# Samples of the expert units: loaded by GpSimd as square blocks and turned by VectorE

## The chip, the cores and the metric

The kernel runs on one core of one Trainium2 chip. The metric is the device time of one execution in microseconds, and every run listed is one execution. A profiled execution shows which engine did what at which time. The engines are TensorE (PE, matmuls, with its weight loads as PEld), VectorE (DVE), ScalarE (ACT), GpSimd (POOL) and SyncE (SP). SP, ACT and POOL also issue DMAs, each through a queue of its own and in the order of its program.

## The reference

The input x holds 128 samples of 64 rows and 256 columns. The layer has three parts.

```python
s0 = relu(x @ swi[0]) @ swo[0]; s1 = relu(x @ swi[1]) @ swo[1]      # two shared experts, 256 -> 1024 -> 256
eo = relu(x @ wi[label]) @ wo[label]                                # one of five experts, by the sample's label
w  = softmax(relu(concat(eo[:,0], s0[:,0], s1[:,0]) @ g1) @ g2)     # a gate from each sample's first row
x  = x + w0*eo + w1*s0 + w2*s1
x  = x + zX*lap_x(x) + zY*lap_y(x) + zR*x*(1-x)                     # differences along columns and rows, per sample
```

All inputs are float32, and so is the result. The labels are only known when the kernel runs.

## The kernel before, in words

**Units.** The 128 samples are sorted by label into 22 units of one expert each: 13 big ones of 8 samples, 5 small ones of 4 and 4 tiny ones of 2, in the order `BBTBBSBTBSBBTBSBSBTBSB`. A table in SBUF (`tab`) gives for each of the 132 places the sample to load, the place to store to, and for each unit the expert. Engines that issue DMAs read it into registers.

**Passes.** `PASSES` lists what TensorE goes through: two short passes with the first rows for the gate (`PRE`), one pass for each unit (`EXP`), then sixteen tiles of 8 samples with two shared experts each (`SH`; `FIRST` is the first of these). A pass has 8 chunks, one for each 128 of the 1024 hidden columns (a tiny unit: 4 chunks, since its first product is made the other way around and turned afterwards). `CHUNKS` numbers them through as g. In chunk g TensorE issues the first product of g (`first_product`, into one of three `hbank`s in PSUM) and then the second product of g-2 (`second_product`, into four `acc`s).

**Precision.** Each product is made from high and low parts: x and the weights are cut into a rounded copy (ScalarE) and the rest (VectorE), and three products are summed. So ScalarE writes XH and VectorE XL for the samples; `cut_high` and `cut_low` do it for the weights, in four pieces of 512 KB a unit (pieces 0 and 1 are halves of wi, 2 and 3 of wo); `hidden_high` and `hidden_low` do it for the hidden activations, in a ring of `NH` = 4 places HH and HL. A piece of raw weights lies in RW[p] until both are done; then GpSimd loads the next unit's piece there (`load_unit`, POOL's queue, pieces in the order 0, 2, 1, 3). `unit_cuts` says at which chunk of which pass each piece is cut: ScalarE at chunk c, VectorE one chunk later.

**Samples of a unit.** SP loads each sample with a DMA of its own into XS, two units ahead (`load_unit_x`), with runs of 4 KB for a big unit. TensorE needs them with the 256 columns on the partitions, so it transposes blocks of 128x128 into a PSUM bank (`transposes`, lines 894 to 913; `tbank`, and accs for unit 0): eight for a big unit in two groups, four for a small one, two for a tiny one. ScalarE copies the bank to XH (`tile_high`, L1127 and L1130) and VectorE subtracts into XL (`tile_low`, L572 and L575). `tile_parts` says at which chunk; the second group waits until VectorE has emptied the bank of the first. XH and XL are double, by the parity of the tile (tile 1+u belongs to unit u).

**Tiles of the shared passes.** Here SP loads each tile in sixteen blocks with runs of 128 bytes so that a 32x32 block transpose on VectorE (`turn_tile`, L585) is all that is needed. ScalarE copies the whole (L1136), VectorE subtracts the whole (L590). `next_tile` says at which chunk.

**Results.** ScalarE and VectorE empty the accs two chunks after a pass (`evacuate`, L1153 and L657 for units), and SP stores each sample to a scratch tensor in HBM, from which it is read back tile by tile in the shared passes. The last unit's odd samples are stored by GpSimd (L1314).

**Order.** Every engine's program is one loop over g with these calls written out by hand. On each engine work is done in the order of the program; a wait holds back all that stands behind it on that engine or queue.

Of the kernel before, what the change touches and what calls it, by code (L numbers as in the profile page):

```python
# [25 lines left out]
NH = 4  # L26
# [7 lines left out]
FIRST_BY = {"ACT": ((1, 0), (1, 1), (1, 2), (1, 3), (2, 0), (2, 1), (2, 2)), "SP": ((1, range(4, 8)), (2, range(3, 8)))}  # L34
# [71 lines left out]
def tile_parts(n, c):  # L106

    if (n, c) == (1, 7):
        return [(1, 0), (1, 1)]
    if n < 2 or n >= FIRST - 1:  # L110
        return []
    tile = tile_of(n) + 1
    if tiny(n):
        return [(tile, 1)] if c == 0 else []
    if tiny(n + 1) and c == 7:
        return [(tile + 1, 0)]
    big = UNITS[tile - 1][1] == 8

    if c == (4 if n == 2 else 3):
        return [(tile, 0 if big else None)]  # L120
    return [(tile, 1)] if c == 6 and big else []
# [18 lines left out]
XT_ORDER = [key for key in T_ORDER if isinstance(key, tuple)]  # L140
XT_AT = {key: i + 1 for i, key in enumerate(XT_ORDER)}

def next_tile(n, c):

    if c != 4 or n < FIRST - 1 or n >= NP - 3:
        return None
    if n == FIRST - 1:  # L150
        return 0
    t, b = PASSES[n][1] // 2, PASSES[n][1] % 2
    return t + 1 if b == 1 else None
# [3 lines left out]


def tile_last(tile):
    return (tile, 1) if (tile, 1) in T_AT else (tile, None)  # L160
# [10 lines left out]
def unit_cuts(n, c):  # L171
    out = []
    if 2 <= n < 1 + NU:
        if tiny(n):
            at = {0: (n + 1, 2)}
        elif tiny(n + 1):

            at = {1: (n + 1, 0), 2: (n + 1, 2), 4: (n + 1, 1), 5: (n + 1, 3), 7: (n + 2, 0)}
        elif n == 2:

            at = {4: (n + 1, 0), 5: (n + 1, 2), 6: (n + 1, 1), 7: (n + 1, 3)}
        else:
            at = {2: (n + 1, 0), 4: (n + 1, 2), 5: (n + 1, 1), 7: (n + 1, 3)}
        if c in at:

            out.append(at[c])
    if 3 <= n <= 1 + NU and tiny(n - 1) and c < 2:
        out.append((n, 1 + 2 * c))
    if c == 3 and n - 2 in SHARED_AT:
        out.append(SHARED_PIECES[SHARED_AT.index(n - 2)])  # L190
    return out
# [42 lines left out]
def cond_resid_program(nc, x, itok, zx, zy, zr, wi, wo, swi, swo, g1, g2, out):  # L234
    eo_d = nc.dram_tensor("eo_scratch", (NS + NSLOT, S, D), F32, kind="Internal").ap()
    ctx = ExitStack()
    with ctx:
# [17 lines left out]
        XS = [sb(f"xs{i}", [128, 4, D]) for i in range(2)]  # L255
        EO = [sb(f"eo{i}", [128, 4, D]) for i in range(2)]
# [50 lines left out]

        hbank = [ctx.enter_context(nc.psum_tensor(f"hbank{i}", [128, 512], F32)) for i in range(HRING)]
# [22 lines left out]
        xb_in = [sem(f"xb_in{i}") for i in range(2)]  # L331
        xz_done = sem("xz_done")
# [24 lines left out]
        HF = RX[:, 256:768].rearrange("p (a n) -> p a n", a=NH)  # L357


        XB, XZ = RW[0:2], RW[2]  # L360

        def unit_cols(a):
            return a[:].rearrange("p (k n) -> p k n", k=2)

        def tile_cols(a, k):
            return a[:].rearrange("p (j k n) -> p j k n", j=4, k=2)[:, :, k, :]
# [36 lines left out]
        def piece_src(a, b, p):  # L403
            return a[:, :, p * 512:(p + 1) * 512] if p < 2 else b[:, (p - 2) * 4:(p - 1) * 4, :]
# [14 lines left out]
        def h_slot(a, g):  # L419

            n, c = CHUNKS[g]
            return a[:, c // 2, c % 2 * 256:(c % 2 + 1) * 256] if n == NP - 1 else a[:, g % NH, 0:h_width(g)]

# [5 lines left out]

        def tile_bank(tile, k):  # L430

            return acc[2 + k] if tile == 1 else tbank
# [12 lines left out]
        for tile in range(1 + NU + NT):  # L445
            x_slot[tile % 2] += 16 * (slots_of(tile - 1)[1] if 1 <= tile <= NU else 1)
            X_VAL[tile] = x_slot[tile % 2]
        st_slot = [0, 0]
# [11 lines left out]
        def _(e):  # L460
# [105 lines left out]
            def tile_low(tile, k):  # L566

                hi, lo = unit_cols(XH[tile % 2]), unit_cols(XL[tile % 2])
                e.wait_ge(t_hi, XT_AT[tile, k])
                if k is None:  # L570
                    w = S * UNITS[tile - 1][1]
                    e.tensor_tensor(lo[:, :, 0:w], tbank[:, 0:2 * w].rearrange("p (k n) -> p k n", k=2),  # L572
                                    hi[:, :, 0:w].bitcast(F32), ALU.subtract).then_inc(t_free, 1)
                else:
                    e.tensor_tensor(lo[:, k, :], tile_bank(tile, k)[:], hi[:, k, :].bitcast(F32),  # L575
                                    ALU.subtract).then_inc(t_free, 1)

            def turn_tile(t):

                if t == 0:  # L580
                    e.wait_ge(*cut_done(1 + NU, 2))
                else:
                    e.wait_ge(xt_lo, t)
                e.wait_ge(xb_in[t % 2], 256 * (t // 2 + 1))
                e.transpose(XZ[:], XB[t % 2][:]).then_inc(xz_done, 1)  # L585

            def tile_low_whole(t):
                tile = 1 + NU + t
                e.wait_ge(xt_hi, t + 1)
                e.tensor_tensor(XL[tile % 2][:], XZ[:], XH[tile % 2][:].bitcast(F32), ALU.subtract).then_inc(xt_lo, 1)  # L590
# [40 lines left out]
            def hidden_low(g):  # L631
# [5 lines left out]
                if PASSES[n][0] == PRE:  # L637
                    e.wait_ge(h_prod, g + 1)
                    e.wait_ge(*h_free(g - NH))
                    e.tensor_scalar(HF[:, g % NH, :], bank[:, 0:128], 0.0, None, ALU.max).then_inc(h_lo, 1)  # L640
                    return
# [133 lines left out]
            for g in range(G + LAG):  # L775
# [5 lines left out]
                if g < G:  # L781
                    for tile, k in tile_parts(n, c):
                        tile_low(tile, k)
                    if next_tile(n, c) is not None:
                        turn_tile(next_tile(n, c))
                    if next_tile(n, c - 1) is not None:
                        tile_low_whole(next_tile(n, c - 1))
# [27 lines left out]
                if g < G and tiny(n):  # L815
                    for ws, p in low_parts_at(n, c):
                        cut_low(ws, p)
# [15 lines left out]
                if g < G and not tiny(n):  # L833
# [39 lines left out]
        def _(e):  # L873
# [20 lines left out]
            def transposes(tile, k):  # L894
                src = XS[tile % 2]
                if (tile, k) != (1, 1):
                    e.wait_ge(t_free, T_AT[tile, k] - 1)
                e.wait_ge(x_in[tile % 2], X_VAL[tile])
                if tile == 1:

                    e.wait_ge(dve_seq, AT["targets"])
                if k is None:
                    js = UNITS[tile - 1][1] // 2
                    for kk in range(2):
                        for j in range(js):
                            at = (kk * js + j) * 128
                            i = e.transpose(tbank[:, at:at + 128], src[:, j, kk * 128:(kk + 1) * 128], ident[:])
                    i.then_inc(t_prod, 1)
                    return
                bank = tile_bank(tile, k)  # L910
                for j in range(3):
                    e.transpose(bank[:, j * 128:(j + 1) * 128], src[:, j, k * 128:(k + 1) * 128], ident[:])  # L912
# [576 lines left out]
```

## Time and profile before

| | |
|---|---|
| runs | 1137.97, 1138.21, 1138.26 us, median 1138.21 |
| the profiled execution | 1138.1 us, its span 1136.6 us |
| busy | PE 99%, PEld 85%, DVE 59%, ACT 40%, POOL 7% |
| DMA queues | SP 59.58 MB in 96706 packets, POOL 50.60 MB in 13952 |
| short passes for the gate | up to 24 us |
| passes of the units | 24 to 405 us |
| shared passes and the end | 405 us to the end |

Busy time counts matmuls from start to modelled end, and they overlap; what one costs is seen from the starts of those around it. Idle time of an engine other than the one that sets the end costs nothing by itself. Where two instructions follow each other on VectorE or ScalarE, the next starts some 0.1 us before the recorded end of the one before.

### The profile page before, as it was taken

The numbers are of one execution on the slowest core, as the hardware profiler recorded it, in microseconds if no ns is written. First come the engines' busy times: TensorE is split into PE (matmuls) and PEld (weight loads), VectorE is DVE, ScalarE is ACT, GpSimd is POOL, SyncE is SP. The second block draws the span as 40 slices with busy tenths as digits, with TensorE's granted clock in tenths as the row PEclk, the third lists the DMA queues.
The fourth block names the chain that finished last, engine by engine and source line by source line (L and its number), as shares of the span: only waits on it lengthen the run. The fifth ranks groups of instructions, "written<-read, shape, count | busy, mean of one in ns | idle before, by whom it ended". The sixth has DMA issues, their size and how long they took to land.

```text
span 1136.6 us, 16584 instructions
## 1 busy us (share of the span) xinstructions
PE 1129.7 (99%) x5956; PEld 962.7 (85%) x5956; DVE 674.2 (59%) x1007; ACT 456.3 (40%) x790; POOL 78.8 (7%) x123
## 2 busy tenths in 40 slices
PE   9999999999999999999999999999999999999998
PEld 8888888888888888888888888888888888888888
DVE  5665667666666635556646555555566465555556
ACT  2554556565565522333333323333333333233233
POOL 1211212111121000000000000000000000000001
PEclk9999999999999999999999999999999999999999
DMA  8555656556665413113023022121130230220200
GB/s 269 174 162 177 190 182 199 180 181 181 177 204 163 115 44 97 24 61 84 19 66 85 11 74 48 47 75 28 58 84 18 66 84 14 72 62 33 75 29 24
DMA packets 111251, 111.82 MB, mean 98 GB/s; under 512 B 78441, under 2 KB 87234, under 8 KB 111170
## 3 DMA queue, kind: packets, MB, share of 16 engines
q1 hardware_dynamic: 96706, 59.58, 19.3%
q0 software_dynamic: 13952, 50.60, 14.8%
q8 instruction: 47, 0.77, 0.3%
q10 hardware_dynamic: 512, 0.59, 0.2%
q14 instruction: 34, 0.28, 0.1%
HBM read 89.40 MB, written 17.04 MB: 94 GB/s over the span
## 4 chain that ended last, share of the span: by engine, by line
PE 96%; DVE 1%; SPq 1%; DMA 1%; issue 0%; ACT 0%; DVEq 0%; ACTq 0%
PE acc L1033 30%; PE hbank L964 15%; PE hbank L965 15%; PE hbank L966 15%; PE acc L1034 15%; SPq L1384 1%; PE tbank L912 1%; PE acc L1019 1%; PE acc L1002 1%; PE hbank L937 0%; DMA rw<-in_L_cond_swi 0%; PE hbank L938 0%; PE acc L1003 0%; PE hbank L980 0%; PE hbank L981 0%
## 5 line engine op out<-in xcount | busy, mean ns | idle before, releaser
L643 DVE SCALAR_TENSOR_TENSOR hl<-hbank,hh 128x512 fp32r<-128x512 f32 (+1 forms) x416 | 271.6, 654 | 410.6 <-ACT hh L1144 410.1
L1144 ACT ACTIVATE hh<-hbank 128x512 fp32r<-128x512 f32 (+1 forms) x416 | 235.7, 568 | 560.3 <-PE hbank L966 557.0
L1033 PE MATMUL acc<-swo,hh 128*128 128x512 f32 x992 | 359.3, 396 | 0.0
L1034 PE MATMUL acc<-swo,hl 128*128 128x256 f32 x992 | 277.8, 280 | 0.0
L1033 PEld LDWEIGHTS acc<-swo,hh 128*128 128x128 f32 x992 | 186.3, 188 | 43.7
L964 PE MATMUL hbank<-xh,swh 128*128 128x512 f32 (+1 forms) x528 | 205.3, 389 | 0.0
L965 PE MATMUL hbank<-xl,swh 128*128 128x512 f32 (+1 forms) x528 | 205.0, 388 | 0.0
L966 PE MATMUL hbank<-xh,swl 128*128 128x512 f32 (+1 forms) x528 | 202.1, 383 | 0.0
L1034 PEld LDWEIGHTS acc<-swo,hl 128*128 128x128 f32 x992 | 187.1, 189 | 9.6
L1033 PE MATMUL acc<-ewo,hh 128*128 128x512 f32 x496 | 180.0, 395 | 0.3 <-DVE hl L643 0.3
L1034 PE MATMUL acc<-ewo,hl 128*128 128x256 f32 x496 | 139.0, 280 | 0.0
L964 PEld LDWEIGHTS hbank<-xh,swh 128*128 128x128 f32 x528 | 99.2, 188 | 23.4
L966 PEld LDWEIGHTS hbank<-xh,swl 128*128 128x128 f32 x528 | 99.4, 188 | 21.6
L1033 PEld LDWEIGHTS acc<-ewo,hh 128*128 128x128 f32 x496 | 93.1, 188 | 21.7 <-DVE hl L643 0.7
L964 PE MATMUL hbank<-xh,ewh 128*128 128x512 f32 (+1 forms) x288 | 107.9, 375 | 0.0
L965 PEld LDWEIGHTS hbank<-xl,swh 128*128 128x128 f32 x528 | 99.2, 188 | 10.1
L965 PE MATMUL hbank<-xl,ewh 128*128 128x512 f32 (+1 forms) x288 | 104.7, 363 | 0.0
L966 PE MATMUL hbank<-xh,ewl 128*128 128x512 f32 (+1 forms) x288 | 104.3, 362 | 0.0
L1034 PEld LDWEIGHTS acc<-ewo,hl 128*128 128x128 f32 x496 | 93.4, 188 | 4.1
L964 PEld LDWEIGHTS hbank<-xh,ewh 128*128 128x128 f32 x288 | 54.2, 188 | 9.7
L966 PEld LDWEIGHTS hbank<-xh,ewl 128*128 128x128 f32 x288 | 54.0, 188 | 9.5
L965 PEld LDWEIGHTS hbank<-xl,ewh 128*128 128x128 f32 x288 | 54.5, 189 | 4.6
(209 smaller groups left out, 972.4 us busy)
## 6 DMA issues: line engine op xcount, KB each, us to landing
rw<-in_L_cond_wi POOLq DMA_DIRECT2D x44, 512.0 KB, 4.5
rw<-in_L_cond_wo POOLq DMA_DIRECT2D x44, 512.0 KB, 4.8
eo_scratch<-eo SPq DMA_DIRECT2D x128, 64.0 KB, 2.2
xs<-in_x SPq DMA_DIRECT2D x16, 512.0 KB, 4.3
rw<-in_x SPq DMA_DIRECT2D x256, 32.0 KB, 2.2
ei<-eo_scratch SPq DMA_DIRECT2D x16, 512.0 KB, 5.5
xs<-in_x SPq DMA_DIRECT2D x125, 64.0 KB, 3.5
out<-ot SPq DMA_DIRECT2D x15, 512.0 KB, 6.3
```

Source lines behind the costliest of these rows:

```text
L643: e.scalar_tensor_tensor(h_slot(HL, g), bank[:, 0:w], 0.0, h_slot(HH, g).bitcast(F32), ALU.max, ALU.subtract).then_inc(h_lo, 1)
L912: e.transpose(bank[:, j * 128:(j + 1) * 128], src[:, j, k * 128:(k + 1) * 128], ident[:])
L964: e.matmul(to, wh[:, k, cs], xh[k], start=(k == 0), stop=False)
L965: e.matmul(to, wh[:, k, cs], xl[k], start=False, stop=False)
L966: i = e.matmul(to, wl[:, k, cs], xh[k], start=False, stop=(k == 1))
L1002: e.matmul(acc[0][:, 0:2 * D], HH[:, g % NH, hs], woc[:, f, :], start=(f == 0), stop=False)
L1019: e.matmul(acc[0][:, 0:D], HF[:, g % NH, :], raw_rows(n, 2 + c // 4)[:, c % 4, :], start=(c == 0), stop=last).then_inc(acc_done if last el ...
L1033: e.matmul(acc[j][:, 0:2 * D], HH[:, g % NH, js], woc[:, c, :], start=(c == 0), stop=False)
L1034: m = e.matmul(acc[j][:, D:2 * D], HL[:, g % NH, js], woc[:, c, 0:D], start=False, stop=last)
L1144: e.activation(h_slot(HU if upright(g) else HH, g), hbank[g % HRING][:, 0:w], ACT.Relu).then_inc(h_hi, 1)
L1384: e.dma_start(to[32 * a:32 * a + 32, :, 32 * q:32 * q + 32], rows[:, :, 32 * a:32 * a + 32]).then_inc(xb_in[t % 2], 16)
```

## The change

- The transposes of units 1 to 21 leave TensorE. Unit 0 keeps them.
- GpSimd loads the samples of units 1 to 21 (`load_samples`), between the pieces 2 and 1 of the weights of the unit before. Each sample becomes 128 partitions of 128 elements: partition 32a + t//2 holds, for its two rows t, the 64 columns of block a. A run in HBM is 256 bytes.
- VectorE turns the unit's samples in 32x32 blocks into a buffer XZ of its own (128 x 1024, `turn_tile`); ScalarE copies from it to XH and VectorE subtracts into XL (`tile_high`, `tile_low`), in four pieces for a big unit and two for others. Each piece sorts the columns (`tile_cols`), so that a sample's rows stand on neighbouring partitions after the second product. `TURN`, `HIGH` and `LOW` say at which chunk.
- With these blocks the 256 columns of x lie in another order over the partitions. The rows of wi and swi are loaded in the same order (`piece_loads`): a piece of wi is two DMAs, one for each k.
- A shared tile's blocks are loaded by SP in four DMAs with runs of 256 bytes, and its copies are two pieces each.
- The stores of a unit go from neighbouring partitions (`sample_rows`), with runs of the same length as before.
- The ring of hidden places has three (`NH` = 3); the last pass gets one more, HHX and HLX.
- Some pieces of weights are cut at other chunks (`unit_cuts`).

```diff
-NH = 4
+NH = 3
+NHF = 4
...
+TURN, HIGH, LOW = {}, {}, {}
+for _n in range(2, 1 + NU):
+    if tiny(_n):
+        continue
+    _tile = tile_of(_n) + 1
+    if _n == 2:
+        _at = (4, 4, 6)
+    else:
+        _at = (2, 3, 5 if tiny(_n + 1) else 7 if blocks(_n) == 4 else 6)
+    TURN[_n, _at[0]] = HIGH[_n, _at[1]] = LOW[_n, _at[2]] = _tile
+    if tiny(_n + 1):
+        TURN[_n, 6] = HIGH[_n + 1, 0] = LOW[_n + 1, 0] = _tile + 1
+for _t in range(NT):
+    _n, _c = (FIRST - 1, 6) if _t == 0 else (FIRST + 2 * _t - 1, 4)
+    TURN[_n, _c] = HIGH[_n, _c] = LOW[_n, _c + 1] = 1 + NU + _t
...
         if tiny(n):
-            at = {0: (n + 1, 2)}
+            at = {2: (n + 1, 2)}
         elif tiny(n + 1):
-            at = {1: (n + 1, 0), 2: (n + 1, 2), 4: (n + 1, 1), 5: (n + 1, 3), 7: (n + 2, 0)}
+            at = {1: (n + 1, 0), 2: (n + 1, 2), 5: (n + 1, 1), 6: (n + 1, 3), 7: (n + 2, 0)}
+        elif blocks(n) == 2:
+            at = {2: (n + 1, 0), 4: (n + 1, 2)}
...
-    if 3 <= n <= 1 + NU and tiny(n - 1) and c < 2:
+    if 3 <= n <= 1 + NU and blocks(n - 1) < 4 and c < 2:
         out.append((n, 1 + 2 * c))
...
+            if size == 8:
+                return [b.rearrange("p (m h s n) -> p h s n m", m=2, h=2, s=8)[:, h, :, :, :] for b in parts for h in range(2)]
...
+            return (flat(XS[tile % 2])[:, 128 * b:128 * b + 128],
+                    x[bass.ds(v, 1), :, :].rearrange("z t (a d) -> (z a) t d", d=64))
...
+                a = a.rearrange("z (a k e) f -> k (z a) e f", k=2, e=32)
+                return [(to[:, k, :], a[k][:, :, p * 512:(p + 1) * 512]) for k in range(2)]
...
+            def turn_tile(tile):
+                if tile > 2:
+                    e.wait_ge(xt_lo, parts_done(tile - 1))
+                if tile <= NU:
+                    w = 2 * tile_width(tile)
+                    e.wait_ge(xu_in[tile % 2], XU_VAL[tile])
+                    e.transpose(XZ[:, 0:w], flat(XS[tile % 2])[:, 0:w]).then_inc(xz_done, 1)
+                    return
...
+            def tile_low(tile):
+                e.wait_ge(xt_hi, parts_done(tile))
+                for lo, both, hi in zip(tile_cols(XL, tile), tile_cols(XZ, tile), tile_cols(XH, tile)):
+                    e.tensor_tensor(lo, both, hi.bitcast(F32), ALU.subtract).then_inc(xt_lo, 1)
...
+            def tile_high(tile):
+                e.wait_ge(xz_done, turned(tile))
                 if tile >= 3:
                     e.wait_ge(h_prod, END[LAST_PASS[tile - 2]])
+                for hi, both in zip(tile_cols(XH, tile), tile_cols(XZ, tile)):
+                    e.activation(hi, both, ACT.Copy).then_inc(xt_hi, 1)
...
+            def load_samples(u):
+                tile = 1 + u
+                s0, k = slots_of(u)
...
+                    e.wait_ge(xz_done, turned(tile - 2))
+                for b in range(k):
+                    e.reg_load(reg, tab[0:1, 0, s0 + b:s0 + b + 1])
+                    v = e.snap(reg, min_val=0, max_val=NS - 1)
+                    e.dma_start(*sample_blocks(v, tile, b)).then_inc(xu_in[tile % 2], 16)
...
             load_unit(0, (2, 1, 3))
-
-            e.wait_ge(h_prod, 18)
+            load_samples(1)
             for u in range(1, NU):
-                load_unit(u, (0, 2, 1, 3))
+                load_unit(u, (0, 2))
+                if u + 1 < NU:
+                    load_samples(u + 1)
+                load_unit(u, (1, 3))
```

## Rows read from the trace of the kernel before

**Rows 1.** The page's busy time of each engine, share of the span, instructions.

```profile
PE 1129.7 (99%) x5956; PEld 962.7 (85%) x5956; DVE 674.2 (59%) x1007; ACT 456.3 (40%) x790; POOL 78.8 (7%) x123
```

**Rows 2.** The page's chain that ended last, share of the span by engine.

```profile
PE 96%; DVE 1%; SPq 1%; DMA 1%; issue 0%; ACT 0%; DVEq 0%; ACTq 0%
```

**Rows 3.** Windows: stretch, length, busy time of each engine, granted clock, DMA share, GB/s.

```profile
24.00:405.00 381.00, 380.68 (x2091) 326.83 (x2090) 242.31 (x342) 212.54 (x349) 67.60 (x92) 1.00 0.59 174
```

**Rows 4.** Groups by line on PE: transposes of samples, count, busy time and mean ns.

```profile
L912 PE MATMUL tbank<-ident,xs 128*128 128x128 f32 x72 | 12.0, 275 | 0.3
...
L913 PE MATMUL tbank<-ident,xs 128*128 128x128 f32 x24 | 6.5, 273 | 0.0
...
L907 PE MATMUL tbank<-ident,xs 128*128 128x128 f32 x28 | 4.5, 271 | 0.0
```

**Rows 5.** Timeline of PE (start, duration): a chunk without and one with transposes.

```profile
150.32 0.28 PE L1034 MATMUL acc<-ewo,hl 128*128 128x256 f32 x1
...
150.68 0.40 PE L965 MATMUL hbank<-xl,ewh 128*128 128x512 f32 x1
...
153.12 0.28 PE L1034 MATMUL acc<-ewo,hl 128*128 128x256 f32 x1
...
153.91 0.39 PE L965 MATMUL hbank<-xl,ewh 128*128 128x512 f32 x1
```

**Rows 6.** The same timeline around the second group, ahead of a tiny pass.

```profile
156.35 0.28 PE L1034 MATMUL acc<-ewo,hl 128*128 128x256 f32 x1
...
157.44 0.39 PE L981 MATMUL hbank<-ewl,xh 128*128 128x512 f32 x1
```

**Rows 7.** Waits of DVE: who waited for whom, us in total, times, longest.

```profile
DVE rw L585 <- DMA rw<-in_x: 3.7, 1, 3.7
```

**Rows 8.** Timeline of DVE in a pass over a small unit.

```profile
125.41 1.42 DVE L657 TENSOR_TENSOR eo<-acc,eo 128x256 f32<-128x256 f32 x4 [0.27 <-ACT eo L1153]
...
128.87 0.41 DVE L643 SCALAR_TENSOR_TENSOR hl<-hbank,hh 128x256 fp32r<-128x256 f32 x1
129.20 1.22 DVE L667 TENSOR_TENSOR ewl<-rw,ewh 128x1024 fp32r<-128x1024 f32 x1
130.33 0.42 DVE L643 SCALAR_TENSOR_TENSOR hl<-hbank,hh 128x256 fp32r<-128x256 f32 x1
```

**Rows 9.** Timeline of PE: first product of the unit after that small one.

```profile
134.84 0.40 PE L964 MATMUL hbank<-xh,ewh 128*128 128x512 f32 x1
```

**Rows 10.** Groups by line on DVE: a strided one and a tiny one.

```profile
L689 DVE TENSOR_SCALAR ss<-y 128x8 f32<-128x8 f32 x15 | 2.5, 166 | 0.0
...
L497 DVE TENSOR_SCALAR ci<-ci 128x5 int32<-128x5 int32 x3 | 0.3, 164 | 0.0
```

**Rows 11.** ACT: one group by line, then its timeline in three places.

```profile
L1136 ACT ACTIVATE xh<-rw 128x1024 fp32r<-128x1024 f32 x16 | 17.0, 1063 | 51.4 <-DVE rw L585 51.4
...
124.99 1.21 ACT L1153 ACTIVATE eo<-acc 128x256 f32<-128x256 f32 x4 [0.31 <-PE acc L1034]
...
152.04 0.60 ACT L1144 ACTIVATE hh<-hbank 128x512 fp32r<-128x512 f32 x1 [1.24 <-PE hbank L966]
...
163.44 1.09 ACT L1144 ACTIVATE hh<-hbank 128x512 fp32r<-128x512 f32 x2
```

**Rows 12.** Groups by line on POOL: issue of a wi piece.

```profile
L1283 POOL DMA_DIRECT2D rw<-in_L_cond_wi x44 | 31.3, 711 | 191.4 <-DVE ewl L667 159.7 <-issue 19.6 <-DVE tab L563 12.0
```

**Rows 13.** Timeline of POOL: first and last of its four stores.

```profile
418.23 0.54 POOL L1314 DMA_DIRECT2D eo_scratch<-eo  x1 [38.90 <-issue]
...
421.54 0.48 POOL L1314 DMA_DIRECT2D eo_scratch<-eo  x1 [0.67 <-issue]
```

**Rows 14.** DMA issues: count, KB each, median us from issue to landing.

```profile
rw<-in_L_cond_wi POOLq DMA_DIRECT2D x44, 512.0 KB, 4.5
...
xs<-in_x SPq DMA_DIRECT2D x125, 64.0 KB, 3.5
...
rw<-in_L_cond_swo SPq DMA_DIRECT2D x2, 512.0 KB, 6.5
```

More of the change, by code:

```diff
@@ L106, in tile_parts @@
 def tile_parts(n, c):
[L108 to L121, printed above, removed]
+    return [(1, 0), (1, 1)] if (n, c) == (1, 7) else []
 T_ORDER = ["counts"]
@@ L139, with turned, parts_done @@
 T_AT = {key: i + 1 for i, key in enumerate(T_ORDER)}
[L140 to L153, printed above, removed]
+TURN, HIGH, LOW = {}, {}, {}
[13 more added lines that the diff above has]
+    TURN[_n, _c] = HIGH[_n, _c] = LOW[_n, _c + 1] = 1 + NU + _t
+def turned(tile):
+    return tile - 1
+def parts_done(tile):
+    return sum(4 if t <= NU and UNITS[t - 1][1] == 8 else 2 for t in range(2, tile + 1))
 LAST_PASS = {tile_of(n): n for n in range(NP)}
-def tile_last(tile):
-    return (tile, 1) if (tile, 1) in T_AT else (tile, None)
 SHARED_PIECES = [(ws, p) for ws in range(2) for p in range(4)]
@@ L331, in cond_resid_program @@
         xb_in = [sem(f"xb_in{i}") for i in range(2)]
+        xu_in = [sem(f"xu_in{i}") for i in range(2)]
         xz_done = sem("xz_done")
@@ L444, in cond_resid_program @@
         X_VAL = {}
-        for tile in range(1 + NU + NT):
-            x_slot[tile % 2] += 16 * (slots_of(tile - 1)[1] if 1 <= tile <= NU else 1)
+        for tile in [0, 1] + list(range(1 + NU, 1 + NU + NT)):
+            x_slot[tile % 2] += 16 * (8 if tile == 1 else 1)
             X_VAL[tile] = x_slot[tile % 2]
+        XU_VAL = {}
+        for tile in range(2, 1 + NU):
+            XU_VAL[tile] = XU_VAL.get(tile - 2, 0) + 16 * UNITS[tile - 1][1]
         st_slot = [0, 0]
@@ L782, in _ @@
                     for tile, k in tile_parts(n, c):
[L783 to L787, printed above, removed]
+                        first_low(k)
+                    if (n, c) in LOW:
+                        tile_low(LOW[n, c])
+                    if (n, c) in TURN:
+                        turn_tile(TURN[n, c])
                 if (n, c) == (2, 5):
@@ L832, in _ @@
                         add_x_last(0)
-                if g < G and not tiny(n):
+                if g < G:
                     for ws, p in low_parts_at(n, c):
@@ L892, in slot_rows, with first_transposes @@
                 e.matmul(tbank[0:1, NSLOT:2 * NSLOT], cols[:, 2:3], msel[:], start=True, stop=True).then_inc(t_prod, 1)
[L894 to L899, printed above, removed]
[L901 to L910 removed]
+            def first_transposes(k):
+                if k == 0:
+                    e.wait_ge(x_in[1], X_VAL[1])
+                    e.wait_ge(dve_seq, AT["targets"])
                 for j in range(3):
[L912 to L913 removed]
+                    e.transpose(acc[2 + k][:, j * 128:(j + 1) * 128], XS[1][:, j, k * 128:(k + 1) * 128], ident[:])
+                e.transpose(acc[2 + k][:, 384:512], XS[1][:, 3, k * 128:(k + 1) * 128], ident[:]).then_inc(t_prod, 1)
             def gate_hidden():
@@ L1063, in _ @@
                     for tile, k in tile_parts(n, c):
-                        transposes(tile, k)
+                        first_transposes(k)
                 if (n, c) == (2, 5):
@@ L1366, in load_tile_x @@
                 if t < 2:
-                    e.wait_ge(t_prod, T_AT[tile_last(tile - 2)])
+                    e.wait_ge(xz_done, turned(tile - 2))
                 else:
```

231 lines of the change are left out of this document (112 added, 119 removed).

## Prediction

> **What bounds the kernel now.** I read the page's busy shares first [rows 1]: TensorE works through 99% of the span, VectorE 59%, ScalarE 40%, GpSimd 7%. Then the chain of work that ended last: 96% of it is TensorE [rows 2]. Then the windows: in the expert passes, 24 to 405 us, TensorE is idle for 0.3 us of 381, at the full granted clock [rows 3]. So time is saved only by taking work off TensorE, and lost only where something becomes late for it. All that the change touches on TensorE lies in that stretch; the 731 us after it keep their matmuls.
>
> **What goes.** TensorE transposes the samples of units 1 to 21: 72, 24 and 28 instructions, 124 in all [rows 4]. Their listed 0.27 us is not their price, since matmuls overlap. I price a group of four by starts [rows 5]: without a group, from the last product of a chunk (150.32) to the second product of the next (150.68) is 0.36 us; with one (153.12 to 153.91) it is 0.79. A group costs 0.43 us, and 124 transposes are 31 groups: 13.3 us. In four places, ahead of the tiny units, TensorE also waits until VectorE has emptied the shared bank: 156.35 to 157.44 [rows 6] is 1.09, less 0.36 and 0.43 leaves 0.30 us, four times 1.2 us. The 0.3 us of idle time comes from the first shared tile's blocks, for which VectorE waited 3.7 us [rows 7] with a hidden half behind it. Four DMAs load them now in place of sixteen, and the turn stands two chunks later: 0.3 us saved (nothing if they land late). Together 14.8 us.
>
> **What three ring places cost.** ScalarE may write chunk g's hidden place when the second product of chunk g-3 is done. TensorE issues that product ahead of chunk g's own first product, for which ScalarE waits anyhow. The same order holds in the last pass with its extra place. Nothing.
>
> **What comes on VectorE and ScalarE.** Per big unit a transpose of 128x1024, priced like the piece of that size (1.13 us from start to start, 129.20 to 130.33 [rows 8]), then four copies of 128x256 on ScalarE and four subtractions on VectorE in place of two of 128x512 each. For four in a row I take ScalarE's evacuation, 1.21 us [rows 11], and VectorE's, 1.42 [rows 8]. In a pass over a big unit (chunks of 2.8 us) this is hidden: a chunk's second product starts 4.2 us after its first has ended, and the two halves of the hidden activation need 1.3 of that. The subtraction at chunk 7 is the close one where a big unit follows a big one (twice): VectorE comes to it 2.6 us after chunk 6's first product, takes 1.4, and the next pass needs it at 4.2.
>
> It is not hidden in the five passes over a small unit, whose chunks last 1.4 us. Take the one after which TensorE starts the next unit at 134.84 [rows 9]; without its two groups it could start at 134.84 - 0.87 = 133.97. VectorE ends the evacuation at 126.83 [rows 8]. Now the transpose stands there (to 128.0), then ScalarE's four copies (129.25) and its hidden half (129.55), then VectorE goes on without a pause: hidden half 0.33 (128.87 to 129.20), a piece 1.13, two hidden halves 0.66, a piece 1.13, the four subtractions 1.42. That ends at 134.25 to 134.4, and the next unit's first product waits for it: 0.4 us, five times 2.0 us. Bounds: nothing, if four copies and four subtractions take what one 128x1024 takes (1.06 [rows 11] and 1.13), and 1.0 each, 5 us, if every piece takes 0.41 by itself, like a hidden half of that size [rows 8].
>
> The copies write in the sorted order, so neighbours in time lie 1 KB apart. No long instruction of the trace does that. The nearest is VectorE's write of each row's two ends, eight elements 1020 bytes apart: 166 ns, against 164 for a tiny one side by side [rows 10]. I take nothing. The upper bound is a doubled time, 1.06 + 1.22 = 2.3 us more a tile [rows 8, 11], which lies on the path in the five small passes, and VectorE's half of it in the two close big ones: 5 x 2.3 + 2 x 1.1 = 13.7 us. The Trainium skill (Advanced Engine Details and Errata, SBUF Cachelines) speaks against my choice: SBUF has lines of 16 bytes, and accesses that go to another line each time are slower. It gives no price, and eight elements are too few to deny it.
>
> **What comes on GpSimd's queue.** 124 sample loads move from SP to POOL, and each piece of wi becomes two DMAs. A piece of 256 runs takes 0.71 us to issue [rows 12]. POOL's only loop with a register for each DMA, the last stores, starts its four in 3.31 us [rows 13]: 1.10 us a step, of which the DMA is 0.5. A sample has 256 runs too, and its 0.71 fits inside: 1.10 us a sample. Bounds: 0.71, and 1.26, the longest step.
>
> Eight samples stand between pieces 2 and 1 of a unit. The tight place is a tiny unit, a big one, a small one (three times). The tiny pass starts one product ahead of 157.44 [rows 6], at 157.1, and ScalarE's pair of hidden halves ends 7.4 us later [rows 11]; now a piece (1.06) stands between them, and with VectorE's half and its piece the cut of piece 2 is done at 10.3. POOL issues the next one: 10.3 + 0.6 + 0.71, then 8 x 1.10 for the samples makes 20.4, and piece 1's second half starts at 21.1. A piece lands 4.5 us after issue [rows 14]; I take that for a half too: 25.6. ScalarE wants it at chunk 5 of the big pass: 6.5 + 5 x 2.8 + 1.4 + 0.7 = 22.6. Late by 3.0 us. ScalarE has 1.24 us to spare in such a chunk [rows 11], and VectorE's subtraction for the small tile (2.6 + 0.7 against 4.2) has 0.9; TensorE stands for the other 0.9 us, three times 2.7 us. Bounds: nothing, with a half landing like a sample of 64 KB (3.5) or samples at 0.71; 6.5, as for a piece in the crowd at the start, and 1.26 a sample make 4.2 each, 12.6 us. By the same reckoning the other pieces are in time or within 0.5 us of it. The Trainium skill (DMA: Bandwidth & Descriptors, Why a DMA increments its semaphore by 16 and not by 1) says that the slowest dimension of the source limits how many of the 16 engines a DMA uses, which makes four for these loads, and that GpSimd's loads take turns over all. Estimated from that, a half lands at some 5.8 us and costs 2.2 three times instead of 0.9, which makes the sum 1131.9. No row shows engines one by one.
>
> Samples are needed a whole pass after they land. Only unit 1's are close (issued from about 22 to 31 us, turned at about 33), and there the hidden half has 2.7 us to spare. Stores keep the length of their runs: nothing.
>
> **Sum.** The profiled execution took 1138.1 us for its span of 1136.6 (the runs' median is 1138.21): 1138.1 - 14.8 + 2.0 + 2.7 = 1128.0 us.
>
> **Rivals.** *All hidden*: small passes and late pieces cost nothing: 1123.3. For it: both terms rest on a few tenths, and the lower bounds reach zero. Against it: VectorE has no gap in the second half of a small pass.
> *Sorted copies are slow*: doubled, 1128.0 + 13.7 = 1141.7; half of that, 1134.9. For it the 1 KB steps, against it the eight elements.
> *GpSimd's queue becomes the bound* (the other side). POOL has from 21 to about 366 us; 21 units of six pieces at 0.71 and one register step of 0.6 are 102, the shared pieces 9. It fails everywhere from (345 - 111) / 124 = 1.89 us a sample. At 2.0 us the loss is 124 x 0.11 = 14 us: 1142; at 2.5 it is 76: 1204. For it: no POOL load with a run this short is in the trace, and the queue is in order, so each late sample holds back a piece, its cut, and TensorE. Against it: 0.71 for as many runs, and 1.26 as the longest step.
>
> **How the numbers follow.** Forecast (1125 to 1131.5) 0.43; all hidden (1122 to 1125) 0.20; slow copies (1131.5 to 1141) 0.20; GpSimd the bound (over 1141) 0.15; below 1122, 0.02. The range 1122 to 1140 leaves out the last two and little more. 0.2% is 2.3 us, about what a measurement tells from no change: faster is below 1135.9. Of the slow copies 0.12 lie below that and 0.08 within. Faster 0.77, same 0.08, slower 0.15.
>
> **What would show it.** The transposes into the shared bank gone and TensorE's busy time near 1115; VectorE's transposes at 1.24 us; sorted copies of 0.3 to 0.45 us each (over 0.55 is the second rival); the first product after a small unit waiting for VectorE's subtraction, 0.4 us, five times; ScalarE waiting some 3 us for a piece of wi, three times; POOL's samples 1.1 us apart. I am wrong if TensorE stands for more than 10 us in all, wherever it is, or if POOL's samples are over 1.5 us apart.

## The result, and the profile after

The changed kernel takes 1173.15 us (median of four runs, 1170.92 to 1182.23) against 1138.09 for the kernel before: a ratio of 1.0325, 95% interval 1.0271 to 1.0379. It is slower by 35 us; the forecast was 1128.0, in a range of 1122 to 1140. The profiled execution took 1173.36 us for a span of 1171.8.

The first lines of the page of the changed kernel, and its chain of waits by engine [rows 1, 2]:

```profile
span 1171.8 us, 16409 instructions
PE 1131.4 (97%) x5832; PEld 956.9 (82%) x5832; DVE 696.9 (59%) x1077; ACT 465.2 (40%) x839; POOL 276.6 (24%) x293
PE 76%; issue 7%; DMA 7%; DVE 3%; POOL 3%; POOLq 2%; ACT 2%; ACTq 0%; DVEq 0%
```

TensorE has its 124 instructions less (5832 for 5956), but it stands idle for 1171.8 - 1131.4 = 40.4 us, and DMAs and GpSimd have come into the chain. The stretch of the unit passes shows where [rows 3]; the columns are the length, each engine's busy time with instructions, the granted clock, the DMA engines' busy share and GB/s:

```profile
24.00:445.00 421.00, 386.64 (x1986) 323.64 (x1985) 266.55 (x402) 221.50 (x385) 262.99 (x261) 0.97 0.77 159
```

34.4 of the 40.4 us are here. The DMA engines are busy for 0.77 of a longer stretch where it was 0.59, for about the same bytes (159 GB/s for 421 us, 174 for 381). The issues and landings of the changed kernel (count, KB each, median us from issue to landing) [rows 14]:

```profile
rw<-in_L_cond_wo POOLq DMA_DIRECT2D x44, 512.0 KB, 8.8
rw<-in_L_cond_wi POOLq DMA_DIRECT2D x84, 256.0 KB, 7.4
eo_scratch<-eo SPq DMA_DIRECT2D x128, 64.0 KB, 3.7
...
xs<-in_x POOLq DMA_DIRECT2D x124, 64.0 KB, 6.2
```

Half a piece of wi lands later (7.4 us) than a whole one did (4.5), and so do wo, which the change did not touch, and the stores. In the kernel before these two were:

```profile
rw<-in_L_cond_wo POOLq DMA_DIRECT2D x44, 512.0 KB, 4.8
eo_scratch<-eo SPq DMA_DIRECT2D x128, 64.0 KB, 2.2
```

GpSimd's samples and the sorted copies, from the groups by line [rows 8, 11, 12]:

```profile
L1330 POOL DMA_DIRECT2D xs<-in_x x124 | 164.8, 1334 | 2.9 <-issue 1.6
L1168 ACT ACTIVATE xh<-xz 128x256 fp32r<-128x256 f32 x58 | 28.4, 626 | 4.1 <-DVE xz L638 4.0
L647 DVE TENSOR_TENSOR xl<-xz,xh 128x256 fp32r<-128x256 f32 x58 | 28.1, 589 | 5.1 <-ACT xh L1168 5.1
```

How one piece becomes late, first on GpSimd's timeline, then on ScalarE's, VectorE's and TensorE's (start, us, instruction, in brackets the wait before it):

```profile
141.52 10.62 POOL L1330 DMA_DIRECT2D xs<-in_x  x8 [0.19 <-issue]
152.14 1.40 POOL L1316 DMA_DIRECT2D rw<-in_L_cond_wi  x2
```

```profile
163.96 1.06 ACT L1216 ACTIVATE ewh<-rw 128x1024 fp32r<-128x1024 f32 x1 [7.07 <-DMA rw<-in_L_cond_wi]
164.93 0.58 ACT L1179 ACTIVATE hh<-hbank 128x512 fp32r<-128x512 f32 x1
```

```profile
165.54 0.69 DVE L700 SCALAR_TENSOR_TENSOR hl<-hbank,hh 128x512 fp32r<-128x512 f32 x1 [6.78 <-ACT hh L1179]
```

```profile
166.28 0.50 PE L1072 MATMUL acc<-ewo,hh 128*128 128x512 f32 x1 [1.65 <-DVE hl L700]
```

Eight samples hold GpSimd for 10.62 us; the halves behind them start at 152.14 and ScalarE gets them at 163.96. ScalarE's wait of 7.07 us holds back the hidden activations behind it, so VectorE waits, and TensorE for the last 1.65 us. ScalarE's waits for wi in the unit passes, 24 to 445 us (us in total, times, longest); in the kernel before there are none there:

```profile
ACT ewh L1216 <- DMA rw<-in_L_cond_wi: 56.3, 20, 7.5
```

The clock adds to it. In three stretches of 5 us from 195 on (same columns as above), TensorE runs short of work, is granted 0.57 and 0.75, the lower of its two levels (1.2 GHz) for part of the time, and the full clock again from 210:

```profile
195.00:200.00 5.00, 3.60 (x19) 2.80 (x18) 0.00 (x0) 0.86 (x1) 4.90 (x5) 1.00 0.94 209
200.00:205.00 5.00, 1.70 (x7) 1.73 (x8) 3.09 (x5) 2.26 (x5) 5.00 (x5) 0.57 1.07 168
205.00:210.00 5.00, 5.00 (x27) 4.45 (x27) 2.83 (x6) 2.02 (x6) 3.94 (x5) 0.75 1.00 109
```

### The profile page after: what moved, and what is told of

It is laid out like the page before. It is cut to its first block, busy times and chain, and to the rows that moved or that the text cites. A ratio compares the mean times of both kernels' runs of the same rounds, so it can differ in the third digit from the quotient of the medians.

```text
span 1171.8 us, 16409 instructions
## 1 busy us (share of the span) xinstructions
PE 1131.4 (97%) x5832; PEld 956.9 (82%) x5832; DVE 696.9 (59%) x1077; ACT 465.2 (40%) x839; POOL 276.6 (24%) x293
## 3 DMA queue, kind: packets, MB, share of 16 engines
q0 software_dynamic: 42272, 59.26, 24.7%
## 4 chain that ended last, share of the span: by engine, by line
PE 76%; issue 7%; DMA 7%; DVE 3%; POOL 3%; POOLq 2%; ACT 2%; ACTq 0%; DVEq 0%
PE acc L1072 24%; PE hbank L1003 13%; PE hbank L1004 12%; PE acc L1073 12%; PE hbank L1005 12%; DMA rw<-in_L_cond_wi 4%; DMA rw<-in_L_cond_wo 2%; POOL xs L1330 2%; POOLq L1328 1%; ACT xh L1168 1%; POOL rw L1316 1%; DVE xl L647 1%; DVE ewl L724 1%; DVE hl L700 1%; ACT hh L1179 0%
## 5 line engine op out<-in xcount | busy, mean ns | idle before, releaser
L1072 PE MATMUL acc<-ewo,hh 128*128 128x512 f32 x496 | 183.5, 401 | 5.8 <-DVE hl L700 4.9
L1380 POOL TENSOR_TENSOR ss<-y 128x254 f32<-128x254 f32 x4 | 2.4, 608 | 694.9 <-DVE y L779 694.9
L1330 POOL DMA_DIRECT2D xs<-in_x x124 | 164.8, 1334 | 2.9 <-issue 1.6
L1003 PE MATMUL hbank<-xh,ewh 128*128 128x512 f32 (+1 forms) x288 | 108.6, 377 | 24.3 <-issue 18.2
```

What stands on the lines that cost most here:

```text
L1003: e.matmul(to, wh[:, k, cs], xh[k], start=(k == 0), stop=False)
L1072: e.matmul(acc[j][:, 0:2 * D], HH[:, g % NH, js], woc[:, c, :], start=(c == 0), stop=False)
L1330: e.dma_start(*sample_blocks(v, tile, b)).then_inc(xu_in[tile % 2], 16)
```

## The experiments: one cost away at a time

Three theories. Q: GpSimd's queue is in order, and eight samples stand ahead of a piece of weights. L: transfers land later by their form and the crowd. C: the sorted copies are slow. Each of the next five runs takes one cost from the changed kernel.

**SP loads the samples.** In SP's loop, as before the change:

```diff
-                if u + 1 < NU:          # GpSimd
-                    load_samples(u + 1)
+                if u + 2 < NU:          # SP, ahead of store_unit(u - 1)
+                    load_samples(u + 2)
```

> The changed kernel, but SP issues the samples' loads (same square blocks in 256-byte runs, same places), in its own queue two units ahead, and GpSimd keeps only weights. The result is the reference's. Theory Q (GpSimd's in-order queue is the bound: 124 samples of 1.33 us stand ahead of weight pieces): with them gone nearly no piece is late, ScalarE's waits for wi fall from 64 us to under 10 and the time to 1125 to 1140. Theory L (pieces land later because of their shape and the crowd of short runs, 7.4 us for a half of wi where a whole took 4.5): the same bytes in the same runs still move at the same time, halves still take about 7 us, and the time stays at 1150 to 1168. Theory C (sorted copies, about 0.6 us for each 128x256): nothing changes on the copies; no more than 10 us come back unless Q is true.

1177.46 us, ratio 1.0349 (1.0331 to 1.0366): no gain, but not for L's reason alone. ScalarE's waits for wi in the unit passes fell from 56.3 to 20.8 us, and a new wait came, VectorE's for samples:

```profile
DVE xz L638 <- DMA xs<-in_x: 55.9, 9, 10.4
```

SP's timeline says why: eight samples take it, in two places, 12.87 and 21.32 us, 1.6 and 2.7 each, where eight in long runs took 7.96 before. Here halves of wi still land in 7.1 us.

**Long runs.** GpSimd keeps its place:

```diff
-                    e.dma_start(*sample_blocks(v, tile, b))
+                    e.dma_start(*sample_rows(XS[tile % 2], u, b, x, v))
```

> The changed kernel, GpSimd still loads the samples at the same place of its queue, but in the old runs (4 KB for a big unit, 2 KB and 1 KB for others), so the columns of a unit's samples are mixed up and the result is another. Theory Q: if GpSimd's time for a DMA goes with its runs, a sample takes 0.5 to 0.8 us in place of 1.33 and the time falls to 1130 to 1145; if it is the same 1.33 us, the time stays above 1160. Theory L: the DMA engines' share falls from 0.8 towards 0.6, landings of wi halves from 7.4 towards 5, and the time falls to 1135 to 1150 even if the queue is as slow. Theory C: no more than 5 us change.

1147.68 us, ratio 1.0087 (1.0052 to 1.0121): 25.5 us back. GpSimd's time for a sample goes with its runs, as Q has it:

```profile
L1330 POOL DMA_DIRECT2D xs<-in_x x124 | 62.1, 501 | 47.5 <-issue 46.4
```

The halves of wi still land late (7.0 us, where L had it towards 5), but they are issued earlier.

**Whole wi.**

```diff
-            if p < 2 and plain:
+            if p < 2:
                 return [(to, a.rearrange("z (k p) f -> p (z k) f", p=128)[:, :, p * 512:(p + 1) * 512])]
```

> The changed kernel with each half of wi and swi as one DMA of 512 KB with the old order of rows (two DMAs before), so the contraction of the first product meets wrong rows and the result is another; bytes and run lengths are the same. Theory L in the form that the shape of these halves makes them slow: landing 4.5 to 5.5 us in place of 7.4 and the time 1140 to 1150. Theory Q: GpSimd saves 0.7 us on each of 42 pieces, 30 us of its queue in all, and the eight samples of 10.6 us still stand ahead of piece 1: half of the loss stays, 1145 to 1158. Theory C: as after, 1165 or more.

1146.43 us, ratio 1.0075 (1.0059 to 1.0092): 26.7 us back, inside the ranges of both L and Q. Not only wi lands earlier (5.3 us), wo does too, 5.7 in place of 8.8, and the stores, 2.8 in place of 3.7. So either the short runs or the four blocks can go, and some 26 of the 35 us go with it. That fits a piece that is late by its delay in the queue and its landing together, less its slack (the time by which it came early before).

**Copies that don't sort**, as many and as large:

```diff
+            if size:
+                return [a[:, i * 2 * w // m:(i + 1) * 2 * w // m] for i in range(m)]
```

> The changed kernel with the units' copies as many and as large as now but from and to neighbouring columns, so a unit's rows come out in another order and the result is another. Theory C: a copy of 128x256 falls from 0.63 and 0.59 us to 0.3 to 0.4, and the time falls by 10 to 15 us, to about 1160. Theories Q and L: TensorE waits for weights and not for the copies: the time falls by 0 to 4 us.

1167.07 us, ratio 1.0264 (1.0232 to 1.0297): 6 us back, between the two theories.

**Samples spread.**

```diff
-                load_unit(u, (0, 2))
-                if u + 1 < NU:
-                    load_samples(u + 1)
-                load_unit(u, (1, 3))
+                for i, p in enumerate((0, 2, 1, 3)):
+                    load_unit(u, (p,))
+                    if u + 1 < NU:
+                        load_samples(u + 1, i)      # a quarter of them
```

> The changed kernel with one thing moved: a unit's samples stand in GpSimd's queue two behind each of the four pieces of weights, and not all eight ahead of piece 1 (one behind each for a small unit). The result is the reference's. Theory Q (the 10.6 us of eight samples in one block make pieces late): the longest delay of a piece falls from 10.6 to 2.7 us, ScalarE's waits for wi fall from 56 us in the unit passes to under 25, the time to 1145 to 1158. Theory L (a half of wi loaded as two DMAs lands in 7 us, whoever loads the samples): the waits stay above 40 us and the time above 1162.

1160.41 us, ratio 1.0209 (1.0192 to 1.0226): 12.7 us back, but ScalarE's waits for wi stay at 51.5 us, and VectorE now waits 24.3 us for samples (2.2 in the changed kernel). Between the theories again.

## The experiments: all away, and a version that is faster

**All suspects away at once:** the last four edits together.

> The changed kernel with all suspects away at once: whole wi in one DMA with the old order of rows, samples in the old long runs, copies from and to neighbouring columns, samples spread behind the pieces. The result is another. If queue, landings and copies are the whole loss, the saving on TensorE shows: 1122 to 1127, with ScalarE's waits for wi under 5 us. If something else that the change brought holds TensorE (three places, VectorE's transposes, the order on ScalarE), the time stays at 1130 or more.

1124.51 us, ratio 0.9885 (0.9869 to 0.9902). The saving on TensorE is there, and nothing else in the change holds more than a microsecond or two of it.

**A version that keeps the result.** Three edits beside the spread samples, the core of them:

```diff
-                a = a.rearrange("z (a k e) f -> k (z a) e f", k=2, e=32)
-                return [(to[:, k, :], a[k][:, :, p * 512:(p + 1) * 512]) for k in range(2)]
+                return [(to, a.rearrange("z (p k) f -> p (z k) f", k=2)[:, :, p * 512:(p + 1) * 512])]
...
+            return (to.rearrange("p (j s d) -> p j s d", s=4, d=64)[b % 2:128:2, :, b // 2, :],
+                    row.rearrange("z t (a d) -> (z a) t d", d=64))      # a sample of a big unit
...
-                    e.transpose(XZ[:, 0:w], flat(XS[tile % 2])[:, 0:w]).then_inc(xz_done, 1)
+                    e.transpose(XZ[:, 0:w // 2], flat(XS[tile % 2])[:, 0:w:2])
+                    e.transpose(XZ[:, w // 2:w], flat(XS[tile % 2])[:, 1:w:2]).then_inc(xz_done, 1)
```

> A version that keeps the idea and takes the three costs away otherwise: channel 2p+k on partition p, so a piece of wi is one DMA with two rows side by side (runs of 2 KB); samples still in 256-byte runs on GpSimd's queue, spread behind the pieces; the sort is in where a sample is put (every other partition for a big unit) and in which partitions are stored, VectorE turns every other column in two transposes, so copies are one contiguous 128x1024 each. The result is the reference's. Theories Q and L: with both gone 1123 to 1132, faster than before. Rival: 256-byte runs alone still cost as much as they seem to in the run with long runs (26 us less than after): 1138 to 1150.

1122.85 us, ratio 0.9870 (0.9854 to 0.9887): 14.2 us faster than the kernel before, with the same runs of 256 bytes. TensorE is never idle in the unit passes:

```profile
24.00:390.00 366.00, 366.00 (x1965) 312.86 (x1964) 258.62 (x375) 209.92 (x336) 207.02 (x215) 1.00 0.69 184
```

**The same with SP's loads.**

> The same version, but SP issues the samples' loads. In the run with SP's samples a sample took 1.6 to 2.7 us of SP's queue, against 1.0 in long runs before, and VectorE waited 56 us for samples. If that came from the crowd that the two DMAs of wi made, it is back to 1.0 to 1.3 here and the time is 1122 to 1130; if it comes from the 256 runs of a sample, VectorE still waits over 20 us for samples and the time is 1140 to 1165.

1133.99 us, ratio 0.9982 (0.9965 to 0.9999). VectorE waits 22.8 us for samples, as the second expectation had it (over 20), though the time is between the two. Without the four blocks beside them SP still takes 1.4 to 1.8 us for each of eight samples. GpSimd is the better place for these loads once they are spread.

## The experiments: each cost put back into the version

**Two DMAs for a piece of wi**, one row a partition each:

```diff
+                a = a.rearrange("z (p k) f -> k p (z f)", k=2)
+                return [(to[:, k, :], a[k][:, p * 512:(p + 1) * 512]) for k in range(2)]
```

> The version (1122.85 us, pieces of wi in one DMA, TensorE idle for 0.0 us from 24 to 450) with one thing put back: each piece of wi is two DMAs of 256 KB, one for each k, where partition p takes row 2p+k (128 runs of 2 KB each, one row a partition). The result is the reference's. If the number of DMAs is what cost 27 us in the changed kernel (0.7 us more of GpSimd's time a piece): landings grow from 5.0 to 6 or more, the time to 1128 to 1145. If it is the form of the source in four blocks of 32 rows: the time stays at 1123 to 1127 and queue 0 keeps some 24 thousand packets.

**Two DMAs from four blocks of 32 rows**, as in the changed kernel (`"z (a k e) f -> k (z a) e f"`, `e=32`):

> The same version with the two DMAs of a piece of wi taken as the changed kernel takes them: for each k four blocks of 32 rows. The contraction meets rows in another order than the samples' columns, so the result is another. If the blocked source is the cause: queue 0 has 42 thousand packets, landings of wi, wo and stores grow to 6.5 to 8 us and 3 us or more, and the time to 1135 to 1155. If the number of DMAs is the cause, it is the same as the run with two plain DMAs.

Two plain DMAs cost nothing: 1122.90 us, ratio 0.9871 (0.9854 to 0.9887). Four blocks: 1153.71 us, ratio 1.0136 (1.0074 to 1.0198), 30.8 us more, with the same weights, runs and number of DMAs. The packets and landings of the two, plain first:

```profile
q0 software_dynamic: 24608, 59.12, 20.0%
...
rw<-in_L_cond_wi POOLq DMA_DIRECT2D x84, 256.0 KB, 3.9
```

```profile
q0 software_dynamic: 42272, 59.26, 26.3%
...
rw<-in_L_cond_wi POOLq DMA_DIRECT2D x84, 256.0 KB, 8.5
```

Not all of the 30.8 us come from late weights. With four blocks the samples land late too, and VectorE's waits for them in the unit passes, 3.8 us in the version, are now:

```profile
DVE xz L639 <- DMA xs<-in_x: 21.3, 6, 8.8
```

**Sixteen and eight blocks** (`e=8` and `e=16`):

> The version with each piece of wi as two DMAs whose source is sixteen blocks of 8 rows (four blocks of 32 rows gave 1153.71 us; two plain halves 1122.9). The contraction meets rows in another order, so the result is another. Theory E (the slowest dimension of the source says how many DMA engines share the transfer; the Trainium skill, DMA: Bandwidth & Descriptors, Why a DMA increments its semaphore by 16 and not by 1, has it so). Worked out from rows: sixteen blocks land like plain halves, 3.9 us, and the time is 1122 to 1126. Theory B (a blocked source makes the transfer slow, however many blocks): landings stay at 8 us and the time at 1140 to 1160, or worse with more blocks.

> The same with eight blocks of 16 rows. The result is another. Theory E: between the two, landings of wi halves 4.5 to 6 us, the time 1123 to 1135. Theory B: as with four blocks, 1140 to 1160.

1122.61 us (ratio 0.9871, 0.9855 to 0.9888) and 1122.94 us (0.9874, 0.9857 to 0.9890). The landings, sixteen blocks first:

```profile
rw<-in_L_cond_wi POOLq DMA_DIRECT2D x84, 256.0 KB, 4.4
```

```profile
rw<-in_L_cond_wi POOLq DMA_DIRECT2D x84, 256.0 KB, 5.3
```

So it is the number of blocks: 8.5 us with four, 5.3 with eight, 4.4 with sixteen, 3.9 with 128 rows. The Trainium skill's rule on engines (DMA: Bandwidth & Descriptors, Why a DMA increments its semaphore by 16 and not by 1) agrees in its order; no run shows the engines one by one. The packets of queue 0 grow as well: 24608 with 128 rows and with sixteen blocks, 30496 with eight, 42272 with four. The extra ones hold 8 bytes each and took 206 of the 1263 us by which the packets of this queue took longer with four blocks; those of 4 KB took 307 ns each in place of 220. Whether fewer engines or something that comes with the extra packets makes the loads late was not told apart. Eight blocks are within the slack, four are not.

**Four blocks in the kernel before**, for the pieces of wi of units 1 to 21 alone:

> The kernel before with one thing of the change: each piece of wi of units 1 to 21 as two DMAs from four blocks of 32 rows. Rows of wi are in another order than the samples' columns, so the result is another. If the blocked source alone makes pieces late: landings of wi grow from 4.5 to 6.5 us or more and the time to 1145 to 1165. If it needs the samples on GpSimd's queue and their short runs: landings grow, but pieces have the slack of the kernel before (some 5 us of waits for a free place each) and the time stays at 1137 to 1141.

1138.13 us, ratio 1.0003 (0.9994 to 1.0013): nothing, although the halves land in 7.4 us, as in the changed kernel. Its landings, then its group of ScalarE's cuts of wi:

```profile
rw<-in_L_cond_wi POOLq DMA_DIRECT2D x84, 256.0 KB, 7.4
```

```profile
L1181 ACT ACTIVATE ewh<-rw 128x1024 fp32r<-128x1024 f32 x44 | 46.4, 1055 | 12.6 <-DMA rw<-in_L_cond_wi 12.4
```

ScalarE waits 12.4 us in all, 8.1 of them for the first piece of all (7.6 in the kernel before), and TensorE never. In this kernel the samples are SP's, their runs long, and the pieces are cut at other chunks. Two more runs tell these apart.

**Four blocks in the version, samples in long runs**, loaded by SP, and then by GpSimd behind the pieces:

```diff
-                    e.dma_start(*sample_blocks(v, tile, b))
+                    e.dma_start(*sample_rows(XS[tile % 2], u, b, x, v))
```

> The version with wi in four blocks (1153.71 us with samples on GpSimd in 256-byte runs), but samples by SP in the long runs of the kernel before; GpSimd loads weights alone. The result is another. If late landings count only with samples in GpSimd's queue or with their short runs beside them: 1122 to 1127, ScalarE's waits for wi under 20 us. If the changed chunks of the cuts took the slack: 1140 or more.

> The same with the samples back on GpSimd's queue, spread behind the pieces, still in long runs (0.50 us each). The result is another. If the queue's time is what adds to the late landing: 8 x 0.5 us spread over four pieces add 1 us to each, and the time is 1124 to 1130. If it is the short runs on the DMA engines: the same as with SP, within 2 us. If neither: 1140 or more.

1125.57 us (ratio 0.9899, 0.9882 to 0.9915) and 1126.19 us (0.9911, 0.9885 to 0.9937), where short runs gave 1153.71. So neither the chunks of the cuts nor the place in the queue makes the late landing count, but the samples' runs of 256 bytes together with the four blocks: without short runs four blocks cost some 3 us, without four blocks the short runs cost nothing (the version). With both, a half lands in 8.5 us and a sample holds GpSimd for 1.13; with long runs on GpSimd's queue these are 7.0 and 0.52, and VectorE's waits for samples fall from 21.3 to 4.4 us. Both readings of the last expectation hold (1124 to 1130, and within 2 us of SP), so the runs do not say which of these decides.

**The samples in one block again**, the spread undone in the version:

> The version with the eight samples of a unit in one block again, ahead of piece 1 of the weights in GpSimd's queue, as in the changed kernel. The result is the reference's. A sample takes 1.13 us there, so piece 1 goes up to 9 us later than without samples. If the block costs what spreading gave in the changed kernel (13 us): 1130 to 1137. If it costs only where pieces also land late: 1123 to 1127.

1133.67 us, ratio 0.9971 (0.9958 to 0.9984): 10.8 us, with pieces of wi that land in 5.3 us. The block costs by itself.

**Sorted copies, the rest away, and the same with copies that don't sort:**

> The changed kernel's sorted copies (four of 128x256 a big unit on ScalarE and on VectorE, 0.63 and 0.59 us each) with the other costs away: whole wi in one DMA with the old order of rows, samples spread behind the pieces. The result is another. The sums of the prediction for the small passes and the two close big ones, with these durations in place of 0.30 and 0.35, give 5 to 10 us: 1128 to 1133 if that working is right. If the copies are hidden beside TensorE: 1123 to 1126. If 256-byte runs at 1.34 us a sample matter by themselves, 1135 or more.

> The run with sorted copies and other costs away (1133.44 us) with the copies from and to neighbouring columns, as many and as large. The result is another. If the sorting of the copies cost its 10.6 us over the version: 1122 to 1126. If it was the samples at 1.34 us in place of 1.13, or the number of copies: 1130 or more.

1133.44 us (ratio 0.9962, 0.9948 to 0.9976) and 1124.76 us (0.9888, 0.9872 to 0.9905): sorting costs 8.7 us. In the first, TensorE's weight loads wait 1.3 us ahead of each of the five units that follow a small one. In the second they wait 0.3 us at the same five places, and in the version at none of them:

```profile
PEld hbank L1006 <- issue: 1.7, 5, 0.3
```

The pieces of the second run:

```profile
L1171 ACT ACTIVATE xh<-xz 128x256 fp32r<-128x256 f32 x58 | 19.6, 407 | 4.4 <-DVE xz L641 4.3
L650 DVE TENSOR_TENSOR xl<-xz,xh 128x256 fp32r<-128x256 f32 x58 | 20.9, 417 | 1.4 <-ACT xh L1171 1.4
```

Against these, the sorted ones take 626 and 589 ns in the changed kernel, 1.5 and 1.4 times as much. What the last run has over the version is 1.9 us. It is not the samples' 1.34 us on GpSimd: the run with all suspects away differs from it in the samples alone (long runs, 0.50 us) and takes 1124.51. The waits above make 1.7 us of it, and they stand behind the copies, which are four pieces in place of one.

Put back one by one, the costs are 30.9 (four blocks), 10.8 (one block of samples), 8.7 (sorting) and 1.9, together 52.3; the changed kernel stands 1173.15 - 1122.85 = 50.3 us over the version. That the two are so close is in part luck, since the costs hang on each other: four blocks cost 30.9 us in the version, some 3 us there without short runs and nothing in the kernel before, and the late samples in the 30.9 are hardly there in the changed kernel. Its TensorE is idle for 34.1 us more (40.4 against 1121.6 - 1115.3 = 6.3) and busy for 16.1 more with the same instructions (1131.4 against 1115.3), which is in part the lower clock after the stalls. The granted clock was at the lower level four times between 80 and 390 us, some 24 us in all; at half the speed that is at most 12 of the 16.1 us (an estimate).

## Why the prediction was wrong, step by step

**What goes, -14.8 us: right.** The version gains 14.2, and 1122.85 is within 0.5 us of the 1123.3 of the case in which all is hidden.

**Three ring places, nothing: right.** The version has them too, and TensorE is idle for 0.0 us in its unit passes.

**A half of wi lands like a whole one, 4.5 us: this step failed.** It measured 7.4, above the upper bound of 6.5, which was the crowd at the start and no bound for a new form. What the sentence on the Trainium skill said, four engines for these loads, was the right warning; the estimate of 5.8 from it was still too low. Other transfers landed late with these (wo 8.8 for 4.8), and the estimate had no term for that. Beside short runs the four blocks, with all that lands late by them, are worth 30.9 us in the version and 26.7 in the changed kernel.

**1.10 us a sample: mis-sized.** It is 1.33, over the longest step of the stores that was taken as upper bound; a store of 16 runs was the model for a load of 256, and the 0.71 of a piece with 256 runs was no guide either. With both measured values the working of the tight place gives: the samples end at 10.3 + 0.6 + 0.71 + 8 x 1.33 = 22.25, the second half starts 0.7 later and lands at 30.35, against 22.6: late by 7.75 us and not by 3.0. The first of the three places in the changed kernel, on GpSimd, ScalarE and TensorE:

```profile
180.26 10.62 POOL L1330 DMA_DIRECT2D xs<-in_x  x8
190.88 1.40 POOL L1316 DMA_DIRECT2D rw<-in_L_cond_wi  x2
```

```profile
199.13 1.06 ACT L1216 ACTIVATE ewh<-rw 128x1024 fp32r<-128x1024 f32 x1 [6.88 <-DMA rw<-in_L_cond_wi]
```

```profile
203.30 0.55 PE L1003 MATMUL hbank<-xh,ewh 128*128 128x256 f32 x1 [4.71 <-issue]
```

At the three places ScalarE waits 6.88, 5.81 and 4.54 us, and TensorE then stands for 4.71, 3.63 and 2.36: 10.7 us for the 2.7 of the sum. The reckoning looked at the right place, and two of its numbers were too small.

**"The other pieces are in time or within 0.5 us of it": this went with them.** Margins that hold at 4.5 and 1.10 fail together: ScalarE waits 20 times for wi in the unit passes, not three, and its longest waits (7.54 us at 69.53, 7.07 at 163.96) are for pieces that were called in time. In the chain that ended last the landings of wi take 4% of the span and those of wo 2%.

**Sorted copies, nothing: wrong, within the bound.** They take 0.63 and 0.59 us, over the 0.55 named for the second rival, and 8.7 us of 13.7 on the path. Eight elements were no evidence; the Trainium skill's sentence against my choice (Advanced Engine Details and Errata, SBUF Cachelines) has the right sign.

**Small passes, 2.0 us: right in place and nearly in size.** Plain pieces take 0.41 and 0.42 us, not 0.30 and 0.35, and with them TensorE's weight loads wait 0.3 us ahead of the five units after a small one, 1.7 us in all, where the forecast was 0.4 each. With sorted copies the same five waits were 1.3 us each.

**The rival that came nearest** is GpSimd's queue as the bound, but not at its point: it was to decide from 1.89 us a sample, by throughput. GpSimd is busy for 263 of the 421 us of the unit passes, not for all of them. What decided was the delay of one piece, queue and landing together, against the slack of that piece.

## What to carry to other kernels

Order the dimensions of a DMA so that the slowest of its source is long: beside short runs, four blocks of 32 rows made a transfer of 256 KB land in 8.5 us where 128 rows took 3.9, and transfers around it landed later too. Whether that costs time depends on the slack: with 7.4 us and long runs the kernel before lost nothing. Put small loads between the large ones of an in-order queue one or two at a time, and price a queue by the delay of its tightest piece, not by its busy share. Sort data by where a DMA puts it or by which partitions a store takes, and keep the copies of the compute engines contiguous.

## What the runs showed of the hardware beyond that

- GpSimd's time for a load of 64 KB was 0.50 us in long runs and 1.33 in 256 runs of 256 bytes; with the destination in other runs (the version) 1.13 in the mean.
- On SP the same short runs took 1.5 to 2.9 us for each of eight samples in the changed kernel and 1.4 to 1.8 in the version, against 1.0 for long ones.
- VectorE's block transposes read every other column at no cost: 705 and 670 ns for 128x512 in the version, 703 from neighbouring columns. Two of them (1375 ns) take longer than one of 128x1024 (1236).
